# Two score matmul streams of a windowed attention, issued in turn instead of one after the other

## The chip, the core and the metric

One core of one Trainium2 chip runs the whole program in one launch. The metric is the device time of that launch in microseconds; the times below are of three runs. The matrix engine is TensorE (PE in the profile, PEld its weight loads), the others are VectorE (DVE), ScalarE (ACT), GpSimd (POOL) and SyncE (SP, which issues DMAs).

## What is computed

Two transformer layers over x of shape (8, 512, 128). The first two thirds of the work are not touched: layer 0 (differential attention and a quantised linear map) and the attention branch of layer 1. The change lies in the feed-forward branch of layer 1, which is itself a small transformer of depth 6 with 16 heads of 64 and windows of 32 tokens:

```python
for i in range(DEPTH):                       # 6
    x = attn_layer(shift_tokens(x), Wqkv[i], ...) + x
    x = ffn_layer(shift_tokens(x), ...) + x

# local_attention: each window of 32 queries sees its own 32 keys and the 32 before
sim = jnp.einsum('bhwie,bhwje->bhwij', bq, bk2) * QK_SCALE
sim = jnp.where(mask, -jnp.finfo(sim.dtype).max, sim)
attn = jax.nn.softmax(sim, -1)
out = jnp.einsum('bhwij,bhwje->bhwie', attn, bv2)
```

Before the scores, queries and keys are brought to unit length, scaled and rotated.

## The kernel before

The depth loop (`l`) holds an attention part and an FFN part. The attention part goes over 32 tiles (8 sequences of 4 tiles of 128 tokens) with a software pipeline of three stages: `slot(front, mid, back, order)` is written out once for every engine, and in one slot the engines do the *back* half of tile n (scores to output projection), the transposes of queries and keys (*mid*) of tile n+1, and the projections (*front*) of tile n+2. `tiles` runs slots in a loop of 7 iterations of 4 slots, with 4 more written out behind it. So a layer has 32 slots with a back half, 192 in all, and the loop turns 6 times in a layer.

TensorE's order within a slot is fixed by hand: the score block (lines 937 to 950), keys of the front tile (L961), transposes of the exponentials in two halves (L967), values (L975), the weighted sums (L983), queries (L989), transposes of the attention output (L997), the transposes of the next tile's queries and keys (L1004), and the output projection (L1009). In each second slot of four it also transposes the next sequence (L912).

The score block works on two groups of 8 heads. In `qT` and `kT` head 2i lies in partitions 0 to 63 and head 2i+1 in 64 to 127, at the same index i. A half `a` writes PSUM bank 7 (a = 0) or bank 5 (a = 1): one mask matmul of 128 rows and 512 columns in bf16 starts the sums (L942), then 8 heads x 4 windows of fp32 matmuls, each 64 rows x 32 columns of weights over 64 keys, add to them (L948). The four windows write four different groups of 32 partitions. The last of a half raises `s_so`.

What follows on the other engines in the same slot. VectorE: for half 0 and then 1, the row maximum out of PSUM (L1168) and the subtraction (L1170); then the front's key cosines (L1151), sines (L1156), norms (L1161), the reciprocals and products that give Y (L1186 to L1190), and at the slot's end the residual (L1208) and then the query cosines (L1151 again). ScalarE: exp of each half (L1074), squares of the keys (L1079), copies of the transposed exponentials (L1083), values (L1090), squares of the queries (L1094), copies of transposes (L1097, L1100, L1103). GpSimd: the inverse norms (L872 to L877) and the sums and scalings of queries and keys (L881 to L888). Each engine takes its own instructions in order, and semaphores join them; TensorE waits for `s_ex` of half c before it transposes half c (L965).

Of the kernel before, what the change touches and what calls it, by code (L numbers as in the profile page):

```python
# [13 lines left out]
P = 128  # L14
# [6 lines left out]
H = 16  # L21
# [10 lines left out]
DH = 64  # L32
INNER = H * DH
WIN = 32
# [45 lines left out]
def program(nc, x, consts, wqkv0, wproj0, wff0, rows0, wqkv1, wo1, wqkv, wo, qkscale, w1, w2, cols, b2, out):  # L80
    with ExitStack() as outer:
        def sb(name, shape, dt=F32, ctx=outer):
            return ctx.enter_context(nc.sbuf_tensor(name, shape, dt))
# [4 lines left out]
        identb = sb("identb", [P, P], BF16)  # L88
        winb = sb("winb", [P, 2, 2 * WIN], BF16)
# [83 lines left out]
        with ExitStack() as ctx:  # L173
# [44 lines left out]
            with ExitStack() as c2:  # L218
                def sem(name):
                    return scoped(c2, name)  # L220
# [464 lines left out]
        with ExitStack() as ctx:  # L685
# [18 lines left out]
            qT = sb("ls_qT", [P, H // 2, P], F32, ctx)  # L704
            kT = sb("ls_kT", [P, H // 2, WIN + T], F32, ctx)
# [32 lines left out]
            s_so, s_mx, s_sub, s_ex = sem("local_scores"), sem("row_max"), sem("less_max"), sem("local_exp")  # L738
# [40 lines left out]
            def banks(i, n=1):  # L779
                return PS[:, i:i + n, :].rearrange("p b n -> p (b n)")  # L780
# [6 lines left out]
            S_BANK, PT_BANK, O_BANK, W_BANK, X_BANK = (7, 5), (7, 4), 5, 0, 1  # L787
# [113 lines left out]
            def _(pe):  # L901
# [7 lines left out]
                with pe.Fori(0, DEPTH) as l:  # L909
# [15 lines left out]
                    def slot(front, mid, back, order):  # L925
# [7 lines left out]
                        if back:  # L933
                            b, t, n = back
                            n, q = l * TILES + n + 1, t % 2

                        if back:
                            pe.wait_ge(s_qte, n)
                            pe.wait_ge(s_kte, n)
                            for a in range(2):  # L940
                                o = banks(S_BANK[a])
                                pe.matmul(o, identb[:, :], winb[:, 0 if t else 1, :].unsqueeze(1).to_broadcast([P, H // 2, 2 * WIN]),  # L942
                                          start=True, stop=False)
                                r = slice(a * DH, a * DH + DH)
                                for i in range(H // 2):
                                    for w in range(NW):
                                        k0 = t * P + WIN * w
                                        ins = pe.matmul(o[WIN * w:WIN * w + WIN, i * 2 * WIN:(i + 1) * 2 * WIN], qT[r, i, WIN * w:WIN * w + WIN],  # L948
                                                        kT[r, i, k0:k0 + 2 * WIN], start=False, stop=(i == H // 2 - 1))
                                ins.then_inc(s_so, 1)  # L950
                        if front:
                            if ft == 0:
                                pe.wait_ge(s_xe, l * B + fb + 1)
# [6 lines left out]
                            for c in range(2):  # L960
                                ins = pe.matmul(banks(K_BANK + c), rows, WQ[:, INNER + c * 512:INNER + c * 512 + 512], start=True, stop=True)  # L961
                            ins.then_inc(s_k, 1)
                        if back:
                            for c in range(2):
                                pe.wait_ge(s_ex, 2 * n - 1 + c)  # L965
                                for i in range(4):
                                    ins = pe.transpose(banks(PT_BANK[c])[:, i * P:i * P + P], PR[:, (c * 4 + i) * P:(c * 4 + i + 1) * P], ident)  # L967
                                ins.then_inc(s_pt, 1)
                        if front:
# [4 lines left out]
                            for e in range(2):  # L974
                                ins = pe.matmul(banks(V_BANK + e), rows, wv[:, e], start=True, stop=True)  # L975
                            ins.then_inc(s_v, 1)
                        if back:
                            pe.wait_ge(s_pte, 2 * n)
                            pe.wait_ge(s_vb[q], windows(l, b, t))
                            for i in range(H // 2):  # L980
                                for w in range(NW):
                                    at = (i % 3) * 2 * (DH + 1)
                                    ins = pe.matmul(banks(O_BANK + i // 3)[WIN * w:WIN * w + WIN, at:at + 2 * (DH + 1)],  # L983
                                                    PRT[:, i * P + WIN * w:i * P + WIN * w + WIN], VB[q][:, w, :, i, :], start=True, stop=True)
                            ins.then_inc(s_o, 1)
                        if front:
                            pe.wait_ge(s_ve, nf)
                            for c in range(2):
                                ins = pe.matmul(banks(Q_BANK + c), rows, WQ[:, c * 512:c * 512 + 512], start=True, stop=True)  # L989
                            ins.then_inc(s_q, 1)  # L990
                        if back:
# [4 lines left out]
                            for i in range(INNER // P):  # L996
                                ins = pe.transpose(banks(Y_BANK, 2)[:, i * P:i * P + P], Y[:, i * P:i * P + P], ident)  # L997
                            ins.then_inc(s_yt, 1)
                        if mid:
                            for a, at, ready, done in ((0, QT_BANK, s_nq, s_qt), (1, KT_BANK, s_nk, s_kt)):  # L1000
                                pe.wait_ge(ready, nm)
                                for i in range(H // 2):
                                    c = a * INNER + i * P
                                    ins = pe.transpose(banks(at, 2)[:, i * P:i * P + P], A[mq][:, c:c + P], ident)  # L1004
                                ins.then_inc(done, 1)
                        if back:
                            pe.wait_ge(s_yte, n)
                            for i in range(INNER // P):
                                ins = pe.matmul(banks(W_BANK)[:, 0:D], YT[:, i * P:i * P + P], WO[:, i, :], start=(i == 0), stop=(i == INNER // P - 1))  # L1009
                            ins.then_inc(s_w, 1)  # L1010

                    tiles(pe, begin, slot, lambda b: None, prep)

                    def ready(p):
# [312 lines left out]
```

## Time and profile before

| | |
|---|---|
| time, median of 3 runs | 5635.59 us (5633.15 to 5646.27) |
| time of the profiled execution | 5633.29 us |
| its span, first to last instruction | 5631.3 us |
| mean granted TensorE clock | 0.903 of full |
| TensorE matmuls busy | 4707.3 us (84%) |
| VectorE busy | 3589.5 us (64%) |
| ScalarE, GpSimd busy | 2466.6 us (44%), 2512.1 us (45%) |

The page shares the span into 40 slices and gives each engine's busy tenths in each. Groups of instructions are listed with their count, their busy time and the idle time of the engine just before them, with what ended it; "issue" says that the engine waited for nothing that the profile shows. The stage with the score block begins at about 1656 us and ends at about 5525 us, with the FFN parts in it. A fp32 matmul leaves two records of its own, each with a weight load. The end of a matmul is modelled, so the starts are what to go by.

### The profile page before, as it was taken

The numbers are of one execution on the slowest core, as the hardware profiler recorded it, in microseconds if no ns is written. First come the engines' busy times: TensorE is split into PE (matmuls) and PEld (weight loads), VectorE is DVE, ScalarE is ACT, GpSimd is POOL, SyncE is SP. The second block draws the span as 40 slices with busy tenths as digits, with TensorE's granted clock in tenths as the row PEclk, the third lists the DMA queues.
The fourth block names the chain that finished last, engine by engine and source line by source line (L and its number), as shares of the span: only waits on it lengthen the run. The fifth ranks groups of instructions, "written<-read, shape, count | busy, mean of one in ns | idle before, by whom it ended". The sixth has DMA issues, their size and how long they took to land. (4 is left out here: it accounts for less than half of the span.)

```text
span 5631.3 us, 144287 instructions
## 1 busy us (share of the span) xinstructions
PE 4707.3 (84%) x58081; PEld 3028.4 (54%) x58081; DVE 3589.5 (64%) x6107; ACT 2466.6 (44%) x3020; POOL 2512.1 (45%) x3540
## 2 busy tenths in 40 slices
PE   3555567776779998899988999799988999889997
PEld 2333322222236666566655666466665666556664
DVE  6665556655646666566756666566666666656675
ACT  2433433443344444444534444344443444434453
POOL 1000011111146664566626666266654666356671
PEclk9888877887789999999999999999999999989999
DMA  0000000000012221222212222122221222122220
GB/s 27 0 0 0 0 1 0 0 0 0 0 47 71 68 67 47 54 67 67 68 30 71 67 67 65 36 67 67 70 61 38 69 71 67 39 54 70 72 66 22
DMA packets 156765, 246.36 MB, mean 44 GB/s; under 512 B 33488, under 2 KB 50896, under 8 KB 155472
## 3 DMA queue, kind: packets, MB, share of 16 engines
q1 hardware_dynamic: 156240, 238.09, 15.9%
q8 instruction: 485, 7.95, 0.6%
q14 instruction: 40, 0.33, 0.0%
HBM read 20.38 MB, written 2.10 MB: 4 GB/s over the span
## 5 line engine op out<-in xcount | busy, mean ns | idle before, releaser
L1151 DVE TENSOR_TENSOR ls_a<-PS,TC 128x1024 f32<-128x1024 f32 x384 | 467.6, 1219 | 424.4 <-ACT ls_r L1079 424.4
L1074 ACT ACTIVATE ls_q<-ls_q 128x512 f32<-128x512 f32 x384 | 242.0, 630 | 891.1 <-DVE ls_q L1170 891.1
L1161 DVE TENSOR_REDUCE ls_ss<-ls_r 128x16 f32<-128x1024 f32 x384 | 466.2, 1214 | 256.6 <-ACT ls_r L1094 256.6
L1156 DVE TENSOR_TENSOR ls_q<-PS,TS 128x512 f32<-128x512 f32 x768 | 491.1, 680 | 19.5 <-POOL ls_a L881 19.5
L948 PE MATMUL PS<-ls_kT,ls_qT 64*32 64x64 f32 x24576 | 483.0, 233 | 6.8 <-issue 6.7
L948 PEld LDWEIGHTS PS<-ls_kT,ls_qT 64*32 64x32 f32 x24576 | 411.4, 117 | 121.3 <-issue 121.1
L381 POOL TENSOR_TENSOR QT<-MXT,ONE 3x512 bf16<-3x512 bf16 x128 | 146.9, 1148 | 729.6 <-ACT MXT L534 722.4
L961 PE MATMUL PS<-WQ,ls_xsT 128*128 128x512 f32 x768 | 453.1, 720 | 16.6 <-issue 15.3
L872 POOL TENSOR_TENSOR ls_nw<-ls_ss,ls_nw 128x32 f32<-128x32 f32 x192 | 48.3, 252 | 925.0 <-DVE ls_rn L1200 925.0
L881 POOL TENSOR_TENSOR ls_a<-ls_a,ls_q 128x1024 f32<-128x1024 f32 x192 | 451.9, 2354 | 15.0
L884 POOL TENSOR_TENSOR ls_a<-ls_a,ls_q 128x1024 f32<-128x1024 f32 x192 | 453.3, 2361 | 0.0
L983 PEld LDWEIGHTS PS<-ls_vb,ls_q 128*32 128x32 f32 x12288 | 338.0, 110 | 150.4 <-issue 74.6
L1094 ACT ACTIVATE ls_r<-PS 128x1024 f32<-128x1024 f32 x192 | 197.1, 1027 | 498.9 <-PE PS L989 498.9
L653 DVE TENSOR_REDUCE mxs<-PS 128x1 f32<-128x512 f32 x512 | 328.2, 686 | 123.3 <-PE PS L416 116.6
L983 PE MATMUL PS<-ls_vb,ls_q 128*32 128x130 f32 x12288 | 392.7, 280 | 8.7 <-ACT ls_q L1083 8.7
L989 PE MATMUL PS<-WQ,ls_xsT 128*128 128x512 f32 x768 | 384.5, 623 | 14.2 <-ACT ls_vt L1090 14.2
L975 PE MATMUL PS<-WQ,ls_xsT 128*128 128x512 f32 x768 | 372.7, 609 | 20.9 <-DVE ls_a L1151 20.9
L1004 PE MATMUL PS<-CT,ls_a 128*128 128x128 f32 x3072 | 371.8, 274 | 14.2 <-POOL ls_a L886 9.6
L1009 PE MATMUL PS<-WO,ls_r 128*128 128x128 f32 x3072 | 377.8, 276 | 6.7 <-ACT ls_r L1097 6.7
L1168 DVE TENSOR_REDUCE ls_mx<-PS 128x8 f32<-128x512 f32 x384 | 263.1, 685 | 178.0 <-PE PS L948 178.0
L886 POOL TENSOR_TENSOR ls_a<-ls_a,ls_rn 128x1024 f32<-128x1024 f32 x192 | 365.3, 1903 | 15.1
L406 PE MATMUL PS<-identb,PT 128*72 128x128 bf16 x2048 | 159.3, 245 | 247.2 <-DVE PT L613 230.7
(215 smaller groups left out, 9400.6 us busy)
## 6 DMA issues: line engine op xcount, KB each, us to landing
ls_vb<-ls_vt SPq DMA_DIRECT2D x1152, 130.0 KB, 2.4
ls_vb<-ls_vt SPq DMA_DIRECT2D x672, 65.0 KB, 2.0
ls_xs<-XL SPq DMA_DIRECT2D x42, 256.0 KB, 4.0
WQ<-wqkv SPq DMA_DIRECT2D x6, 1536.0 KB, 6.6
ls_vb<-ls_vz SPq DMA_DIRECT2D x96, 65.0 KB
WO<-wo SPq DMA_DIRECT2D x24, 128.0 KB, 6.3
X<-x SPq DMA_DIRECT2D x8, 256.0 KB, 4.5
out<-X SPq DMA_DIRECT2D x8, 256.0 KB, 3.5
```

Source lines behind the costliest of these rows:

```text
L881: pool.tensor_tensor(a4[:, 1], a4[:, 1], b4[:, 1], ALU.add).then_inc(s_ck, 1)
L884: pool.tensor_tensor(a4[:, 0], a4[:, 0], b4[:, 0], ALU.add).then_inc(s_cq, 1)
L948: ins = pe.matmul(o[WIN * w:WIN * w + WIN, i * 2 * WIN:(i + 1) * 2 * WIN], qT[r, i, WIN * w:WIN * w + WIN], kT[r, i, k0:k0 + 2 * WIN], sta ...
L961: ins = pe.matmul(banks(K_BANK + c), rows, WQ[:, INNER + c * 512:INNER + c * 512 + 512], start=True, stop=True)
L975: ins = pe.matmul(banks(V_BANK + e), rows, wv[:, e], start=True, stop=True)
L983: ins = pe.matmul(banks(O_BANK + i // 3)[WIN * w:WIN * w + WIN, at:at + 2 * (DH + 1)], PRT[:, i * P + WIN * w:i * P + WIN * w + WIN], VB[q ...
L989: ins = pe.matmul(banks(Q_BANK + c), rows, WQ[:, c * 512:c * 512 + 512], start=True, stop=True)
L1004: ins = pe.transpose(banks(at, 2)[:, i * P:i * P + P], A[mq][:, c:c + P], ident)
L1009: ins = pe.matmul(banks(W_BANK)[:, 0:D], YT[:, i * P:i * P + P], WO[:, i, :], start=(i == 0), stop=(i == INNER // P - 1))
L1151: nc.vector.tensor_tensor(v4(A[fq])[:, a], src, tab, ALU.mult).then_inc(done, 1)
L1156: ins = nc.vector.tensor_tensor(v4(SW)[:, a, :, lo:lo + h2], src[:, :, hi:hi + h2], TS[:, ft, a, lo:lo + h2].unsqueeze(1).to_broadcast([P, ...
L1161: nc.vector.tensor_reduce(ss[:, fq, a * H:a * H + H], v4(SQ)[:, a], AX.X, ALU.add).then_inc(done, 1)
```

## The change

The mask matmuls of both halves are issued first. Then the loop over heads is outside and the loop over the two halves within it: 4 windows of half 0, 4 of half 1, then the next pair of heads. Each half raises `s_so` after its last matmul, as before.

```diff
                             for a in range(2):
-                                o = banks(S_BANK[a])
-                                pe.matmul(o, identb[:, :], winb[:, 0 if t else 1, :].unsqueeze(1).to_broadcast([P, H // 2, 2 * WIN]),
+                                pe.matmul(banks(S_BANK[a]), identb[:, :], winb[:, 0 if t else 1, :].unsqueeze(1).to_broadcast([P, H // 2, 2 * WIN]),
                                           start=True, stop=False)
-                                r = slice(a * DH, a * DH + DH)
-                                for i in range(H // 2):
+                            for i in range(H // 2):
+                                for a in range(2):
+                                    r = slice(a * DH, a * DH + DH)
                                     for w in range(NW):
                                         k0 = t * P + WIN * w
-                                        ins = pe.matmul(o[WIN * w:WIN * w + WIN, i * 2 * WIN:(i + 1) * 2 * WIN], qT[r, i, WIN * w:WIN * w + WIN],
-                                                        kT[r, i, k0:k0 + 2 * WIN], start=False, stop=(i == H // 2 - 1))
-                                ins.then_inc(s_so, 1)
+                                        ins = pe.matmul(banks(S_BANK[a])[WIN * w:WIN * w + WIN, i * 2 * WIN:(i + 1) * 2 * WIN],
+                                                        qT[r, i, WIN * w:WIN * w + WIN], kT[r, i, k0:k0 + 2 * WIN],
+                                                        start=False, stop=(i == H // 2 - 1))
+                                    if i == H // 2 - 1:
+                                        ins.then_inc(s_so, 1)
```

## Rows read from the trace of the kernel before

**Rows 1.** The page: busy time by engine, and TensorE's tenths of 40 slices.

```profile
PE 4707.3 (84%) x58081; PEld 3028.4 (54%) x58081; DVE 3589.5 (64%) x6107; ACT 2466.6 (44%) x3020; POOL 2512.1 (45%) x3540
...
PE   3555567776779998899988999799988999889997
```

**Rows 2.** Score matmuls: the page's group, then durations ns (min/median/max) of the line.

```profile
L948 PE MATMUL PS<-ls_kT,ls_qT 64*32 64x64 f32 x24576 | 483.0, 233 | 6.8 <-issue 6.7
...
L948 PE MATMUL PS<-ls_kT,ls_qT x24576: 216/216/313, 1656.5 to 5512.1; 64*32 64x64 f32 x200
```

**Rows 3.** Timeline of one tile from 2410.64: start us, us, engine, line [idle before].

```profile
2410.64 0.38 PE L942 MATMUL PS<-winb,identb 128*128 128x512 bf16 x1
2410.95 1.10 PE L948 MATMUL PS<-ls_kT,ls_qT 64*32 64x64 f32 x64
2410.98 0.29 DVE L1208 TENSOR_TENSOR XL<-PS,XL 128x128 f32 x1 [0.66 <-PE PS L1009]
2411.19 1.21 DVE L1151 TENSOR_TENSOR ls_a<-PS,TC 128x1024 f32<-128x1024 f32 x1
...
2412.32 0.68 DVE L1168 TENSOR_REDUCE ls_mx<-PS 128x8 f32<-128x512 f32 x1
...
2413.32 1.98 PE L961 MATMUL PS<-WQ,ls_xsT 128*128 128x512 f32 x4
...
2415.07 0.63 ACT L1074 ACTIVATE ls_q<-ls_q 128x512 f32<-128x512 f32 x1 [0.69 <-DVE ls_q L1170]
2415.14 1.27 PE L967 MATMUL PS<-CT,ls_q 128*128 128x128 f32 x8
...
2421.29 0.41 DVE L1190 TENSOR_TENSOR ls_r<-PS,ls_rc 128x256 f32<-128x256 f32 x1
2421.85 0.41 PE L997 MATMUL PS<-CT,ls_r 128*128 128x128 f32 x2
```

**Rows 4.** Timeline of the next tile: its first matmul, and VectorE's first maximum.

```profile
2426.72 0.38 PE L942 MATMUL PS<-winb,identb 128*128 128x512 bf16 x1
...
2428.20 0.69 DVE L1168 TENSOR_REDUCE ls_mx<-PS 128x8 f32<-128x512 f32 x1 [0.17 <-PE PS L948]
```

**Rows 5.** All waits: engine and line, what for, us in total, times, longest us.

```profile
PE PS L942 <- issue: 83.0, 36, 2.8
```

**Rows 6.** Timelines of two tiles that follow a turn of the loop.

```profile
2391.35 0.38 PE L942 MATMUL PS<-winb,identb 128*128 128x512 bf16 x1 [2.01 <-issue]
...
2392.82 0.69 DVE L1168 TENSOR_REDUCE ls_mx<-PS 128x8 f32<-128x512 f32 x1 [1.91 <-PE PS L948]
...
2393.00 0.68 PE L948 MATMUL PS<-ls_kT,ls_qT 64*32 64x64 f32 x19
...
2394.41 1.50 PE L948 MATMUL PS<-ls_kT,ls_qT 64*32 64x64 f32 x45 [0.74 <-issue]
2395.84 0.50 PEld L961 LDWEIGHTS PS<-WQ,ls_xsT 128*128 128x128 f32 x2 [0.17 <-issue]
...
2529.51 0.38 PE L942 MATMUL PS<-winb,identb 128*128 128x512 bf16 x1 [2.51 <-issue]
2529.81 1.93 PE L948 MATMUL PS<-ls_kT,ls_qT 64*32 64x64 f32 x64
...
2534.08 3.21 PE L961 MATMUL PS<-WQ,ls_xsT 128*128 128x512 f32 x4
2537.12 1.04 PE L967 MATMUL PS<-CT,ls_q 128*128 128x128 f32 x8
```

**Rows 7.** Busy time by stretch, with the granted clock (PEclk).

```profile
2410.60:2458.10 47.50, 47.47 (x768) 33.61 (x767) 35.49 (x57) 25.33 (x32) 35.19 (x52) 1.00 0.30 79
2461.60:2468.20 6.60, 6.50 (x104) 3.94 (x94) 2.76 (x4) 1.26 (x2) 6.52 (x4) 0.50 0.01 2
...
2529.50:2548.00 18.50, 18.49 (x254) 13.14 (x255) 10.57 (x17) 8.09 (x10) 9.58 (x10) 0.82 0.16 42
2598.10:2618.20 20.10, 20.10 (x254) 14.10 (x255) 10.63 (x17) 8.21 (x10) 9.50 (x9) 0.75 0.13 34
```

## What the change does to the time: the prediction

> **What bounds the kernel now.** I read the page first, then the costliest groups, then a timeline of one attention tile in the last stage, and last the tiles after a loop turn. TensorE is busy 84% of the span, and 9 tenths or more in the stage where the change lies [rows 1]; the local score matmuls (L948) are its largest group there, 483 us [rows 2]. That makes the change look promising, and the timeline says otherwise. The reader is to see in [rows 3] that two things are full at once in a tile of about 15.6 to 16.1 us. TensorE issues without a hole: score block (two mask matmuls L942, two halves of L948) from 2410.64 to 2413.32, 2.68 us, then keys L961, and so on. Beside it runs a loop that holds no score matmul: the residual L1208 waits for the output projection L1009 of the tile before; VectorE then does L1151 (query cosines), the first maximum L1168, subtraction L1170, L1168, L1170, back to back; ScalarE's second exponential ends at 2415.70; and only then can TensorE transpose the second half (L967) and go on to L975. L967 lasts 1.27 us there against 1.04 us in [rows 6] where nothing is waited for: 0.23 us of it are the wait for that exponential. On VectorE the same exponential leads through L1079, L1151 and the rest to L1190, which ends at 2421.70, just before L997 starts at 2421.85. So the score block and the loop are level.
>
> **The change, part by part.** Instructions, operands and sums stay the same: 2 L942 and 64 L948 (128 records, as fp32 takes two each) a tile. Only order moves.
>
> (a) Both L942 come first. Before, each costs 0.31 us from its start to that of the first L948 [rows 3]. Full-array bf16 matmuls of 512 columns that follow each other need not let the array run empty between them; 512 columns are four times L948's pair of passes over 64 (55 ns, below), so about 0.22 us. So the first L948 comes at 0.22 + 0.31 = 0.53 us instead of 0.31. The flag for VectorE's first half can't come until that half is done.
>
> (b) The 64-row halves alternate. The trace shows how closely column tiles overlap: 64 records in 1.10 us, of which the last takes 0.22 [rows 2, 3]: 0.88 us, 16 groups of four at 55 ns. At the half clock it is 1.93 - 0.31 = 1.62 us, 101 ns or so a group [rows 2, 6]. It doubles with the clock period, so a group is bound by what streams through the array, not by the issue of instructions. Row halves in turn are nowhere in this trace. Bounds: they overlap fully, all 128 records in 0.88 us; or not at all, 1.76 us. Below nothing is not excluded either, but four column tiles already overlap freely with no cost for changing tile, so I take none. I take the full overlap, since the nearest row (column tiles at one half) shows four of four overlapping. The Trainium skill ("TensorEngine Tiling (Array Packing)", Key Properties) also says that tiles run independently, and that only a change of mode drains the engine; no run here shows it for row tiles.
>
> (c) The first flag moves. Before, the last record of the first half starts at 0.31 + 0.88 = 1.19 us of the tile; with full overlap at 0.53 + 0.88 = 1.41, 0.22 later. In the tile at 2426.72 the maximum waits 0.17 us for the flag and starts at 1.48; in the tile at 2410.64 it starts at 1.68 without waiting, since VectorE comes from L1151 [rows 3, 4]. So it has 0.20 us of slack there, which the 0.22 uses up. The second flag comes 1.1 us sooner but VectorE is still at the first half: worth nothing.
>
> **The sum for full overlap.** TensorE leaves the block 2.68 - 1.56 = 1.1 us sooner (0.53 + 0.88 + 0.15 for the last to drain = 1.56), does the keys, and then waits for the second exponential, whose time the loop pins. In the 150 tiles that don't follow a loop turn the gain is nothing. About 48 of them (those like 2426.72) have the flag 0.22 late; half or more of it is taken by the slack before L975 and L997, I take 0.08: 48 x 0.08 = 4 us lost; 12 tiles at the layers' ends, without new queries and keys, are a plain chain of latencies: 12 x 0.2 = 2 us lost.
>
> The other 42 tiles come after a turn of the loop: 36 where TensorE's first matmul waits for something the profile doesn't show, 83.0 us in all [rows 5], and the 6 first of the layers. Here the clock was granted at half (1.2 GHz) for some 7 us after that wait of 2.0 to 2.5 us [rows 6, 7] (0.50 from 2461.60 to 2468.20), and the block sets the pace: 4.49 us from 2391.35 to 2395.84. But part of that is again a wait for nothing shown: after 64 + 19 records L948 stops and goes on at 2394.41, 3.06 us after the tile's start [rows 6]. I read both waits as instructions being fetched after the jump; the change has as many instructions, so the point stays at about 3.06, the faster order only reaches it sooner, and the remaining 45 records take 45 / 8 x 107 ns = 0.6 us rather than 1.2. The block ends at about 3.06 + 0.6 + 0.15 = 3.8 us instead of 4.49: 0.7 gained. In a turn without a second stop (4.57 us from 2529.51 [rows 6]) the stop would appear, at about 2.9, and the gain is near the same. VectorE's first maximum slips from 1.47 to about 4.0 us of the tile; with 0.69 x 4 + 0.63 the second exponential ends near 7.4, where TensorE has just done the keys (L961, 3.21 us at mostly half clock [rows 6]: 3.8 + 3.3 = 7.1). So I take 0.6 of 0.7: 36 x 0.6 = 22 us; for the 6 first tiles 0.5 each, 3 us. Sum: -22 - 3 + 4 + 2 = -19 us on the profiled 5633.3 us, 5614; that execution lies 2.3 us under the median, so **5616 us**. FFN and the two attentions before are untouched. Between full overlap's own ends, 5590 (the fetched instructions come as soon as they are wanted) and 5640.
>
> **Rivals.** Break-even: 150 tiles x d us of a later flag eat 19 us at d = 0.13, a group of eight at 63 ns rather than 55. So a little missing overlap turns the sign.
>
> *Partial overlap.* Sixteen instructions must pass in 55 ns, where the trace shows eight; if issue or PSUM writes hold the eight tiles to 1.5 times the old pace, the records take 1.17 us, the flag is another 0.29 late, and 150 x 0.29 = 44 us are lost, with turns gaining 0.4 x 36 = 14 and the 6 us above: about 5635.6 + 44 + 6 - 14 = 5672. The skill's measured packing of four row tiles ("TensorE: Matmul & The Clock Gate", Part 3: 3.07 times for four) points this way.
>
> *No overlap: slower.* The halves share the array in turn; the block shrinks by one drain at most, and the first flag comes after 30 of 32 groups: 0.53 + 30 x 0.055 = 2.18 instead of 1.19, 0.99 later, less 0.20 slack where VectorE was late: about 0.8 in 150 tiles, 120 us, less some 5 at the turns: 5750. Each tile's loop runs through L1168, so all of it counts. For it: nothing in the trace has shown two row groups at once; against: the free overlap of column tiles. The same skill page (Part 1) says that matmuls never start closer than about 25 ns; the trace shows 0.88 us / 64 = 14 ns [rows 3], so the trace disagrees, but a floor just under 14 would give this rival's time.
>
> *The clock.* TensorE idles 1.1 us more in every tile, and after a turn it also stops for almost 2 us at the fetch. After the 2.0 to 2.5 us waits the granted clock fell to half; the tile at 2598.10 had it longer (mean 0.75, 20.1 us) than the one at 2529.50 (0.82, 18.5 us) [rows 7]: 1.6 us a time. If all 36 turns went so, 58 us: 5674. Against: the 1.0 of the whole stretch 2410.60 to 2458.10 holds small waits too, none of 1 us though.
>
> **How the numbers follow.** Full overlap 0.40, partial 0.28, none 0.25, clock 0.07. Likeliest: 5616, a hair over 0.3% under the median, and 0.3% (17 us) is about what a measurement of this kernel can tell from no change. Full overlap splits 0.24 faster, 0.14 same, 0.02 slower; the light end of partial overlap gives 0.03 faster and 0.12 same, the rest 0.13 slower; none is slower; the clock case is 0.02 same, 0.05 slower. Faster 0.27, same 0.28, slower 0.45. The likeliest case is a small gain while the cases of a loss hold more chance together, so the range must reach both: 5590 to 5755, leaving out the lower tail of the first case and the upper of the others, under 2 in 10.
>
> **What would show it.** Right: L948 (new line) with 128 records in one row of about 1.1 us at full clock; L1168 starting 1.65 to 1.7 us after the first L942 in every warm tile; the wait of L967 for ScalarE's exponential grown by about 1.1 us; tile lengths still 15.6 to 16.1. Partial or none: that row at 1.4 to 2.0 us, L1168 waiting for TensorE in all tiles, tiles of 16.0 to 16.9. Clock: more stretches granted at half. Wrong altogether: tiles shorter than 15.5 us, which would mean the loop through VectorE isn't what I take it for, or a block after turns that doesn't stop at the 84th record.

## The result and the profile after

Before and after ran in turn, five times each. The median went from 5635.59 us (5625.54 to 5651.88) to 5681.4 us (5674.48 to 5682.55), a ratio of 1.0072 with a 95% interval of 1.0051 to 1.0093: slower by 0.7%, 46 us, where the forecast was 5616. The profiled execution took 5675.67 us, its span is 5673.7 against 5631.3.

The page of the kernel after, to be read beside [rows 1]: busy time of the engines, then two groups of the list (busy us, mean ns | idle before, by releaser). The line numbers have moved by two: L948 is still the scores, L941 the masks, L963 the keys, L969 the transposes of the exponentials, L1170 the maximum, L1076 the exponential.

```profile
PE 4579.6 (81%) x58081; PEld 2885.5 (51%) x58081; DVE 3590.5 (63%) x6107; ACT 2463.7 (43%) x3020; POOL 2511.3 (44%) x3540
...
L1170 DVE TENSOR_REDUCE ls_mx<-PS 128x8 f32<-128x512 f32 x384 | 263.1, 685 | 246.6 <-PE PS L948 246.2
...
L969 PE MATMUL PS<-CT,ls_q 128*128 128x128 f32 x1536 | 257.4, 295 | 156.8 <-ACT ls_q L1076 153.7
```

TensorE did its work in 128 us less and the kernel got longer: it now waits 153.7 us for exponentials, and VectorE waits 246.6 us for scores, where it was 178.0 before. One tile shows how. The timeline of the kernel after, of the tile that answers to [rows 3] (start us, us, engine, line, [idle before]), and the maximum of the next one, that answers to [rows 4]:

```profile
2413.50 0.59 PE L941 MATMUL PS<-winb,identb 128*128 128x512 bf16 x2
...
2414.03 1.79 PE L948 MATMUL PS<-ls_kT,ls_qT 64*32 64x64 f32 x128
...
2415.74 1.98 PE L963 MATMUL PS<-WQ,ls_xsT 128*128 128x512 f32 x4
2415.76 0.69 DVE L1170 TENSOR_REDUCE ls_mx<-PS 128x8 f32<-128x512 f32 x1 [0.50 <-PE PS L948]
...
2417.89 0.66 PE L969 MATMUL PS<-CT,ls_q 128*128 128x128 f32 x4 [0.17 <-ACT ls_q L1076]
...
2419.21 0.65 PE L969 MATMUL PS<-CT,ls_q 128*128 128x128 f32 x4 [0.67 <-ACT ls_q L1076]
...
2430.18 0.59 PE L941 MATMUL PS<-winb,identb 128*128 128x512 bf16 x2
2430.70 1.49 PE L948 MATMUL PS<-ls_kT,ls_qT 64*32 64x64 f32 x128
...
2432.16 0.69 DVE L1170 TENSOR_REDUCE ls_mx<-PS 128x8 f32<-128x512 f32 x1 [0.68 <-PE PS L948]
```

The block, from the first mask to the first key matmul, takes 2.24 us instead of 2.68 in the first of them and 2.05 in the second, so TensorE is earlier at the keys. But VectorE's first maximum comes 2.26 us and 1.98 us after the tile's start, where it was 1.68 and 1.48, and everything behind it follows; TensorE gives its gain back as a wait at L969.

Two more places. The tile after a loop turn that answers to the ones of [rows 6], and what it waits for in total (the view of waits: us, times, longest), both of after:

```profile
2464.76 0.59 PE L941 MATMUL PS<-winb,identb 128*128 128x512 bf16 x2 [2.37 <-issue]
2465.28 1.06 PE L948 MATMUL PS<-ls_kT,ls_qT 64*32 64x64 f32 x83
2467.79 0.94 PE L948 MATMUL PS<-ls_kT,ls_qT 64*32 64x64 f32 x45 [1.46 <-issue]
2468.66 3.05 PE L963 MATMUL PS<-WQ,ls_xsT 128*128 128x512 f32 x4
```

```profile
PE PS L941 <- issue: 78.5, 36, 2.7
...
PE PS L948 <- issue: 41.7, 36, 1.8
```

And the last tile of a layer, which has no keys, values or queries to put into the waits. First the stretches of that tile in the kernel after, then that tile in two layers of the kernel before (stretch, length, busy time (count) of PE, PEld, DVE, ACT, POOL, granted clock, DMA share, GB/s):

```profile
2856.30:2863.40 7.10, 3.65 (x154) 2.58 (x155) 2.96 (x5) 2.34 (x4) 0.00 (x0) 1.00 0.01 2
2863.40:2866.80 3.40, 3.04 (x60) 2.58 (x50) 0.27 (x3) 0.00 (x0) 0.00 (x0) 0.50 0.02 5
...
2870.20:2873.60 3.40, 3.25 (x15) 3.25 (x16) 0.00 (x0) 0.09 (x1) 0.00 (x0) 0.50 0.00 0
```

```profile
2184.30:2199.00 14.70, 9.19 (x228) 7.23 (x225) 4.96 (x12) 3.36 (x5) 0.00 (x0) 1.00 0.01 2
2850.30:2868.60 18.30, 13.20 (x228) 10.44 (x225) 4.96 (x12) 3.36 (x5) 0.00 (x0) 0.72 0.01 2
```

Before, this tile is 14.7 us long in four layers and 18.3 in the two in which the clock was granted at half (1.2 GHz) in it. After, it falls in all six, and the tile takes 18.2 to 19.8 us.

Where the 42.4 us of span come from, tile by tile. A tile is measured from its first mask matmul to the next one's, and grouped by its place in the loop of four:

| tiles | number | mean before, us | mean after, us | total, us |
|---|---|---|---|---|
| after a loop turn, or first of a layer | 42 | 19.03 | 17.92 | -46.7 |
| second of four | 42 | 16.09 | 16.56 | +20.0 |
| third of four | 42 | 15.61 | 16.12 | +21.3 |
| fourth, with the wait of the turn | 36 | 18.10 | 18.31 | +7.6 |
| fourth, no turn behind it | 6 | 15.63 | 15.96 | +2.0 |
| next to last three of a layer | 18 | 15.78 | 16.44 | +11.8 |
| last of a layer | 6 | 15.9 | 19.0 | +18.6 |
| FFN parts, and where the stage starts | | | | +8 |

The first row holds two kinds. The 36 tiles after a turn went from 19.06 to 18.16 us, 32 us in all; the six first of a layer from 18.87 to 16.46, 14.5 us in all. Of these six, four ran their whole score block at the half clock in the profile of before and three in that of after, so a part of the 14.5 us is the clock.

### The profile page after: what moved, and what is told of

Read it like the earlier page. It is cut to its first block and busy times, and to the rows that moved or that the text cites. A ratio compares the mean times of both kernels' runs of the same rounds, so it can differ in the third digit from the quotient of the medians.

```text
span 5673.7 us, 144287 instructions
## 1 busy us (share of the span) xinstructions
PE 4579.6 (81%) x58081; PEld 2885.5 (51%) x58081; DVE 3590.5 (63%) x6107; ACT 2463.7 (43%) x3020; POOL 2511.3 (44%) x3540
## 3 DMA queue, kind: packets, MB, share of 16 engines
q1 hardware_dynamic: 156240, 238.09, 15.9%
## 5 line engine op out<-in xcount | busy, mean ns | idle before, releaser
L1076 ACT ACTIVATE ls_q<-ls_q 128x512 f32<-128x512 f32 x384 | 241.8, 630 | 965.1 <-DVE ls_q L1172 965.1
L963 PE MATMUL PS<-WQ,ls_xsT 128*128 128x512 f32 x768 | 431.2, 689 | 20.0 <-issue 14.0
L1170 DVE TENSOR_REDUCE ls_mx<-PS 128x8 f32<-128x512 f32 x384 | 263.1, 685 | 246.6 <-PE PS L948 246.2
L991 PE MATMUL PS<-WQ,ls_xsT 128*128 128x512 f32 x768 | 386.1, 626 | 14.1 <-ACT ls_vt L1092 14.1
L977 PE MATMUL PS<-WQ,ls_xsT 128*128 128x512 f32 x768 | 372.5, 608 | 20.9 <-DVE ls_a L1153 20.9
L969 PE MATMUL PS<-CT,ls_q 128*128 128x128 f32 x1536 | 257.4, 295 | 156.8 <-ACT ls_q L1076 153.7
L1011 PEld LDWEIGHTS PS<-WO,ls_r 128*128 128x128 f32 x3072 | 368.1, 196 | 8.3 <-ACT ls_r L1099 8.3
L886 POOL TENSOR_TENSOR ls_a<-ls_a,ls_rn 128x1024 f32<-128x1024 f32 x192 | 365.4, 1903 | 15.0
L888 POOL TENSOR_TENSOR ls_a<-ls_a,ls_rn 128x1024 f32<-128x1024 f32 x192 | 365.1, 1902 | 0.0
```

The costliest lines, as they stand in the source:

```text
L886: pool.tensor_tensor(a4[:, 0], a4[:, 0], scale(0), ALU.mult).then_inc(s_nq, 1)
```

## The experiments

Unless it says otherwise a ratio is against the kernel before, with its 95% interval. "First maximum" is VectorE's first row maximum of a tile, counted from that tile's first mask matmul; warm tiles are the second, third and fourth of each four, which run at the full clock; the three numbers are means over the second, third and fourth tiles of four (before: 1.68, 1.47, 1.66 us; after: 2.14, 2.01, 1.98).

**1. The late flag alone.** The kernel before, with its order of matmuls, but half 0 raises its flag only from the first head of half 1:

```diff
-                                ins.then_inc(s_so, 1)
+                                    if a and i in (0, H // 2 - 1):
+                                        ins.then_inc(s_so, 1)
```

> The order of before; only the flag for half 0 is raised later, by the first head of half 1, about 0.58 us after its own last matmul (the changed kernel's first maximum starts 0.33 to 0.54 us later than before's). TensorE's work is untouched. Theory (the first flag's lateness goes straight into a loop through VectorE, tile after tile): first maximum at about 2.05 us of every tile instead of 1.47 to 1.68, tiles 0.4 to 0.45 us longer, 150 tiles: 60 us, so 5690 to 5700. Rival (the loss comes from how TensorE takes its instructions, the clock or the fetch after a turn, and VectorE has room): within 15 us of before.

5735.46 us, ratio 1.0182 (1.0160 to 1.0205). TensorE's stream is that of [rows 3], and only VectorE moves (timeline of this kernel; L1169 is its maximum):

```profile
2577.86 0.38 PE L942 MATMUL PS<-winb,identb 128*128 128x512 bf16 x1
2578.17 1.10 PE L948 MATMUL PS<-ls_kT,ls_qT 64*32 64x64 f32 x64
...
2579.90 0.69 DVE L1169 TENSOR_REDUCE ls_mx<-PS 128x8 f32<-128x512 f32 x1 [0.28 <-PE PS L948]
```

The first maximum is at 2.04 us in all three classes, that is 0.36, 0.57 and 0.39 later, and the tiles are 0.38, 0.55 and 0.40 us longer (16.46, 16.16, 16.03). So a later first flag alone makes the loss, one to one, with no cushion. It costs more than the whole change because after turns it loses 13 us (19.33 us a tile) where the change gains 47; the last tile fell to the half clock in all six layers in both. The loss was larger than the 55 to 65 us that I expected: of the 112 us between the profiled executions 74 lie in the 186 tiles ahead of the layers' last, 19 in the last tiles, 12 in the FFN parts, and 7 are a stage that began later.

**2. The masks first, the halves still one after the other.**

```diff
                                           start=True, stop=False)
+                            for a in range(2):
+                                o = banks(S_BANK[a])
                                 r = slice(a * DH, a * DH + DH)
```

> Part one of the change alone: both mask matmuls first, then the halves one after the other. Theory: the first flag comes 0.22 us later, which is the 0.20 us of slack; TensorE leaves the block 0.2 us sooner: within 15 us of before, tiles of 15.6 to 15.7 us. Rival (two masks in front already cost the 45 us): 5670 or more.

5650.06 us, ratio 1.0028 (1.0014 to 1.0043). The first maximum is at 1.69 us everywhere: unchanged where VectorE was late anyway, 0.21 later in the third tile of four, which got 0.19 longer (15.80). The turn tiles (with the first of each layer) got 0.63 shorter (18.40) with no row half beside another: more than half of the gain of the change there (1.11) comes from the masks alone. The time is at the edge of the 15 us that I expected, and what holds it up lies elsewhere: the last tile of a layer fell to the half clock in all six layers here too, and the last four tiles of the layers cost 24 us more than before.

**3. Two heads of half 0 for one of half 1**, so that the first flag comes earlier than in the change, with some overlap kept:

```diff
+                            at = [0, 0]
+                            for a in (0, 0, 1, 0, 0, 1, 0, 0, 1, 0, 0, 1, 1, 1, 1, 1):
+                                i = at[a]
+                                at[a] += 1
```

> Both masks first, then two heads of half 0 for one of half 1 until half 0 is done, then the rest of half 1. Same instructions. Theory (after TensorE's queue of ready instructions is used up, matmuls come about 8 ns apart, which is enough for half 0 at full pace and a part of half 1): half 0 is done at 1.4 to 1.5 us of the tile, first maximum at 1.7 to 1.75, block end as with the change (keys at 1.95 to 2.05 us); the gain after loop turns stays; 5610 to 5640. Rival (alternating row halves slows half 0 whatever the ratio): first maximum at 1.9 or later, 5660 or more.

5644.16 us, ratio 1.0022 (1.0008 to 1.0037). First maxima 1.83, 1.77, 1.76; tiles 16.25, 15.89, 15.74; turn tiles 18.12. All of it lies between experiment 2 and the change, as it must if only the place of the first flag and the length of the block count. The 186 tiles ahead of the layers' last add up to 9 us less than before; the last tiles took it back, with 17.9 to 18.9 us in five layers and 16.2 in one. The first maximum was to come at 1.7 to 1.75 us and the time to be 5640 at most, so this is a near miss.

**4. VectorE's query cosines ahead of the residual**, in the kernel before, so that VectorE is free sooner:

```diff
+                        if front:
+                            cosines(0, Q_BANK, s_aq)
                         if back:
                             dve.wait_ge(s_w, n)
...
-                        if front:
-                            cosines(0, Q_BANK, s_aq)
```

> The order of before on TensorE; on VectorE the query cosines of the front tile go ahead of the residual, in whose wait for TensorE (0.63 to 0.66 us) they fit. Theory (loop through VectorE): the first maximum no longer comes behind the cosines and starts at about 1.47 us in every tile instead of 1.68 in two of three; L967 no longer waits; TensorE's own work is then the bound at about 15.4 to 15.5 us a tile: 10 to 25 us faster than before. Rival (TensorE alone bounds): within 5 us.

5629.33 us, ratio 0.9996 (0.9981 to 1.0012): no change in time, where I expected 10 to 25 us. The first maximum is at 1.47 us in all tiles, the second tile of four is 0.16 shorter, the fourth 0.14, the third the same: where the maximum comes sooner the tile is shorter, which is the converse of experiment 1. The 186 tiles together are 28 us shorter in the profiled execution, but its stage began 22 us later than in that of before and the last tile fell to half clock in three layers instead of two. Where the stage begins differs by up to 44 us between profiled executions of kernels whose work up to there is the same, so only the tiles carry this reading, not the total.

**5. The key matmuls between pieces of the score block.** Does the array or the supply of instructions limit the block? The change, with one key matmul after the first two pairs of heads and one after the next two; all the work is the same:

```diff
+                                if front and i in (2, 4):
+                                    c = i // 2 - 1
...
+                                    ins = pe.matmul(banks(K_BANK + c), rows, WQ[:, INNER + c * 512:INNER + c * 512 + 512], start=True, stop=True)
```

> The changed kernel with the two key matmuls of the front tile put into the block: one after the heads i = 0 and 1 of both halves (32 score matmul records), one after i = 2 and 3 (32 more), the rest behind. It tells two causes of the slow second part of the block apart. Theory (instructions come about 8 to 9 ns apart once the ready ones are used up; while a key matmul of 0.86 us runs, ready ones pile up again): each of the first two parts and the first 32 records of the third start within 0.24 us, as the first 32 do in the changed kernel. Rival (row halves hinder each other after the start, in PSUM or in reading): the second and third parts show 0.28 us or more for 32. The time of the whole is of no interest, since the flags come later: 5700 or more.

It is far slower (6251 us in its one execution); VectorE waits 605.2 us for scores there. What it is for is the pace (timeline of this kernel: L962 scores, L955 keys):

```profile
2506.91 0.45 PE L962 MATMUL PS<-ls_kT,ls_qT 64*32 64x64 f32 x32
2507.29 1.13 PE L955 MATMUL PS<-WQ,ls_xsT 128*128 128x512 f32 x2
2508.35 0.45 PE L962 MATMUL PS<-ls_kT,ls_qT 64*32 64x64 f32 x32
2508.73 1.13 PE L955 MATMUL PS<-WQ,ls_xsT 128*128 128x512 f32 x2
2509.79 0.86 PE L962 MATMUL PS<-ls_kT,ls_qT 64*32 64x64 f32 x64
```

By the starts of the records, the first 32 after a long matmul begin within 0.238 us, in all three places and in all 126 warm tiles: mostly 6 to 7 ns apart, 8 records per 55 ns, full overlap of the row halves. The last 32 of the third piece take 0.40 us. In the change the same: the first 32 records begin within 0.238 us, and the next three lots of 32 take 0.37, 0.31 and 0.35 (medians), so that 128 begin within 1.27 us instead of 0.88 (in the second tiles of four, as the one at 2413.50 above, within 1.39). As the same heads go fast when a long matmul stands before them and slow when other score records do, neither the array nor the writes to PSUM limit them. What is used up is a stock of 32 records with their 32 weight loads; I read it as TensorE running ahead of its instructions. The Trainium skill ("TensorE: Matmul & The Clock Gate", Architectural detail: the array is 16× 32×32, not 1× 128×128) gives TensorE's queue as 64 instructions; the 32 + 32 in the fast stretch agree. How it is filled up again stays open: a stock that is filled at the later pace (about 11 ns a record) while it is used at 6.9 ns should last for more records than it holds, and no run shows why the pace falls right behind the 32nd.

**6. The last two tiles of a layer filled.** The change, with mask matmuls into a bank that nobody reads, 25 in the last tile and 21 in the one before, in the places where TensorE waits:

```diff
+                                for _ in range(k):
+                                    pe.matmul(banks(V_BANK), identb[:, :], winb[:, 0, :].unsqueeze(1).to_broadcast([P, H // 2, 2 * WIN]),
+                                              start=True, stop=True)
...
+                                fill((8, 3)[c])
```

> The changed kernel; in the last two tiles of each layer, which have no new keys, values and queries, TensorE runs mask matmuls into a PSUM bank that nobody reads while it would wait (8, 3, 3, 7 and in the last tile 4). The output is the same. Theory (about 30 of the 42 us lost lie at the layers' ends, because TensorE's idle pieces there grew from 0.9 to 2.1 us and the clock was granted at half in all six layers instead of two): no half clock from tile 30 to the end of tile 31, last tile to FFN 14.8 to 15.5 us instead of 18.2 to 19.8: 5650 to 5660. Rival (the half clock there comes whatever TensorE does): 5675 to 5690.

5652.3 us, ratio 1.0039 (1.0024 to 1.0053): 29 us under the change by the two medians, about 19 by the two ratios, each against the kernel before at its own time. More work for TensorE, and the last tile went to 15.2 us in all six layers, at 2.4 GHz throughout (stretch of this kernel that answers to 2856.30 to 2873.60 above):

```profile
2855.40:2870.60 15.20, 14.07 (x253) 8.88 (x251) 4.94 (x12) 3.36 (x5) 0.00 (x0) 1.00 0.01 2
```

The warm tiles are as in the change (16.59, 16.13, 15.97). The last four tiles of the layers are 37 us shorter than in the change; experiment 9 tells how much of that is the change's own. So most of the layer ends' loss is the clock, and TensorE's idle time there is what brings it.

**7. Small masks.** To take the masks' cost off the path: experiment 3's order and 4's cosines, and the masks as eight matmuls of 64 rows and 32 columns behind one short full one, so that they overlap as the scores do:

```diff
+                            pe.matmul(banks(S_BANK[0])[:, 0:2 * WIN], identb[:, :], winb[:, 0, :], start=True, stop=True)
...
+                                for w in range(NW):
+                                    r = slice(a * DH, a * DH + DH)
+                                    pe.matmul(banks(S_BANK[a])[WIN * w:WIN * w + WIN], identb[r, a * DH:a * DH + WIN],
```

> Built from the two-to-one order: the two mask matmuls of 128 rows become eight of 64 rows x 32 columns on the same eight tiles as the scores (behind one short full-array matmul that takes the wait), so nothing drains between masks and scores and both masks stream at once; and VectorE's query cosines go ahead of the residual. Theory: the first flag comes at about 1.25 us, first maximum at about 1.5 us in every tile (before: 1.47 to 1.68), keys at 1.8 to 1.9 us; warm tiles of 15.4 to 15.6 us, the gain after turns stays (about 1 us in 42 tiles): 5580 to 5610. Rival (mask matmuls on small tiles bring back a mode change or use up the ready instructions): first maximum at 1.8 or later and 5640 or more.

5624.14 us, ratio 0.9978 (0.9965 to 0.9990). The first score record starts at 0.35 us instead of 0.53, the last at 1.82 instead of 2.02; first maxima 1.60, 1.56, 1.56; tiles 16.03, 15.67, 15.54. I expected 5580 to 5610. Two things are missing: the last tile fell to the half clock in five layers of six, and the turn tiles gained 0.68 us (18.35), not 1.

**8. Small masks and filled ends** (7 and 6 together).

> The small-mask kernel (two heads of half 0 for one of half 1, small masks, cosines ahead of the residual) with the last two tiles of each layer filled as in the run before. Theory: its own last tile cost 18.4 us in five layers of six, as the changed kernel's; filling takes it to 15.2 us and tile 30 from 16.2 to 15.0: 20 to 28 us less than 5624, so 5596 to 5605. Rival (filling helps only where the masks of 512 columns stand together): 5615 or more.

5598.99 us, ratio 0.9942 (0.9925 to 0.9959). Halves in turn are part of a faster kernel once the flag is held early and the layer ends are kept from the half clock. Whether the mixed order adds anything to it isn't shown: no run has the small masks and the early cosines with the halves one after the other, and experiment 2, where the halves follow each other, already took the turn tiles to 18.40.

**9. The kernel before with filled ends.**

> The kernel before with the same filling. It tells how much of the 29 us that filling gave the changed kernel is the change's own loss. Theory (before had the half clock in the last tile in two layers of six in its profile, and a short stretch in tile 30 in all): 6 x 0.9 us in tile 30 and about 2 x 3.6 less: 5620 to 5628. Rival (filling is worth the same everywhere, so the layers' ends are no part of the change's loss): 5600 to 5610.

5623.1 us, ratio 0.9980 (0.9969 to 0.9990). The filling alone is worth 0.2% where two of six ends had fallen: 11 us in the last four tiles of the layers. With the ends filled in both, the change (experiment 6) is only 5 us longer there than the kernel before, against 30 without. The other 0.4% of experiment 8 belong to the block and the cosines together.

**10. The loop of seven turns written out**, in the kernel before, on all engines:

```diff
-                with eng.Fori(0, B - 1) as g:
+                for g in range(B - 1):
```

> The kernel before with the loop over 7 x 4 tiles written out, so that no engine jumps within a layer; instructions and waits are otherwise the same. It tests what the waits with no releaser after a turn are. Theory (instructions are being fetched after the jump): neither the 2.0 to 2.5 us before the first mask nor the stop after 83 score records come any more, the clock stays full through a layer: 36 x (2.5 + 3.4) = 210 us less: 5410 to 5440. Rival (the waits belong to a sequence's first tile, not to the jump): within 1% of before.

5426.68 us, ratio 0.9623 (0.9605 to 0.9642). No wait of L942 for issue is left of the 83.0 us of [rows 5], turn tiles and fourth tiles take 15.98 and 15.51 us instead of 19.03 and 18.10, and TensorE is busy without a hole in the middle of a layer (stretch of four tiles that begins where a turn was; the last column but two is the clock):

```profile
2455.50:2518.00 62.50, 62.48 (x1022) 44.58 (x1021) 47.28 (x76) 33.29 (x42) 46.63 (x69) 1.00 0.28 74
```

So the stops after a turn were the jump's. That they are instructions which weren't there yet is a reading; for it speaks that the second stop comes behind the 83rd record in either order of the block. The Trainium skill ("Runtime: NRT & Kernel Launch", Instruction fetch mechanics) says that a taken branch breaks the sequential prefetch, and that the engine stalls when the target isn't in the stretch of instructions already fetched; the trace agrees, with 36 waits of up to 2.8 us, the second stop, and the half clock they bring.

**11. Everything together**: 8 with the loop written out.

> All of it together: small masks in the two-to-one order, cosines ahead, last tiles filled, loop written out. With no turns left the change's gain there (about 1 us in 42 tiles) is gone too, and what stays is the warm tile of 15.5 to 15.6 us: about 25 to 35 us under the written-out kernel (192 x 0.08 and the layers' ends): 5385 to 5410.

5429.14 us, ratio 0.9627 (0.9608 to 0.9646). I expected 25 to 35 us under experiment 10; it is the same. The view of waits of this kernel names a new one, where experiment 10 has none on its score line, and the timeline shows it (L964 scores, L954 small masks, L979 keys):

```profile
PE PS L964 <- issue: 24.8, 20, 1.7
```

```profile
2457.54 0.41 PE L954 MATMUL PS<-winb,identb 64*32 64x512 bf16 x8
2457.76 1.66 PE L964 MATMUL PS<-ls_kT,ls_qT 64*32 64x64 f32 x120
2461.00 0.32 PE L964 MATMUL PS<-ls_kT,ls_qT 64*32 64x64 f32 x8 [1.58 <-issue]
```

The block stops after 108 to 122 records for 1.1 to 1.9 us, in the tiles 9, 10, 22 and 23 (counted from 0) of nearly every layer, the same places in the code each time, and the keys stop once more for 1.1 to 1.4 us in tile 8 of all six. There is no jump there. By the same reading the faster block runs out of instructions in a straight line too. The second, third and fourth tiles of four get longer than those of experiment 10 (the second 16.32 against 15.95), which eats what the layer ends gain (last tile 14.8 us in all six against 18.2 in three of six).

## Why the prediction was wrong

The step that failed is (b), the full overlap of the two row halves: 128 records in 0.88 us were forecast, and 1.27 us were measured. It makes the first flag late, and the step behind it, (c), priced a late flag too low. Together the warm tiles cost 51 us instead of 4; with the flag where full overlap would have put it (experiment 2) they cost 10. A second term failed beside them: the layers' last tiles, put at 2 us, cost 30.

**The bound: right.** TensorE and a loop through VectorE are level, and the block's length isn't what a warm tile hangs on. Experiments 1 and 4 moved the first maximum alone, later and sooner, and the tiles followed; in the change the block got 0.6 to 0.75 us shorter in the median of each class (0.44 in the tile shown) and the tiles longer. TensorE's wait at L969 is where the gain went, as said: 0.84 us in the tile shown against 0.23 before, so grown by 0.6 and not by 1.1.

**(a) The masks first: right.** The first score record starts at 0.525 us in the warm tiles of after, 0.53 was said.

**(b) The overlap: the failed step.** I took all 128 records in 0.88 us because a group "is bound by what streams through the array, not by the issue of instructions". That holds at half clock, where 128 records of the first tiles begin within 1.75 us, 8 per 107 ns; and for the first 32 records at full clock. From there something else binds, by experiment 5 neither the array nor PSUM, and the 128 records take 1.27 us. The row used for the inference, column tiles at the old pace, was bound by what streams while it asks for half as many instructions in a nanosecond; it said nothing on the double. The rival of partial overlap named the issue of instructions as a cause (with PSUM writes, which it isn't), took 1.5 times the old pace (1.17 us) and gave 5672. Measured are 1.39 times the old pace and 5681; that the two times lie so near is partly luck, since this rival had neither the layer ends nor the larger gain at the turns in its sum.

**(c) The flag: sized far too small.** It was to come 0.22 later, of which VectorE's lateness would take 0.20, and only 48 tiles would lose 0.08. It came so that the first maximum is 0.46, 0.54 and 0.33 later in the three classes, and the tiles are 0.48, 0.51 and 0.34 longer. Two things are in it: (b)'s 0.39 us, and the missing cushion. Experiment 2, whose flag is the one that I forecast, cost the third tile of four 0.19 for 0.21, not 0.08. The "slack before L975 and L997" that I had read out of [rows 3] doesn't exist. In the warm tiles the sum said +4 and it was +51 (20.0, 21.3, 7.6 and 2.0). About 10 of them are the price of the flag at full overlap (experiment 2); the other 41 come with the missing overlap.

**The turns: right in kind, too small in size.** The block after a turn stops after 83 records; in the tile shown it goes on 3.03 us after the tile's start (forecast 83, about 3.06) and is over at 3.90 (3.8), in others between 3.4 and 4.2. As forecast the second stop appeared where there was none: 14 of the 36 turns had it before, all 36 have it after. And the order buys only what lies between the stops. But each of the 36 tiles gained 0.90 us, not 0.6, and the six first of a layer 2.4, not 0.5: their half clock also got shorter, 4.2 us a tile over the 42 instead of 7.4. Of the 36, 5 had none at all, 13 had 3.4 us and 18 had 6.8, where before 30 had 6.8 and six 10.2. Why the clock was granted sooner isn't shown. The stretch of half clock that answers to the second row of [rows 7] is 3.4 us long here and begins 2.7 us after the tile's start instead of ahead of most of its block (stretches of after):

```profile
2464.70:2467.40 2.70, 1.58 (x85) 1.02 (x85) 0.00 (x0) 0.00 (x0) 2.60 (x3) 1.00 0.03 8
2467.40:2470.80 3.40, 3.01 (x48) 1.80 (x49) 2.03 (x4) 0.63 (x1) 3.32 (x3) 0.51 0.03 5
```

So -46.7 against the forecast's -25. The rival on the clock had this place the wrong way round. That the waits are the jump's, which I had only read, experiment 10 shows; that they are its fetch stays a reading.

**The layer ends: next to nothing in the sum.** I gave the last two tiles of each layer 0.2 us each, as a plain chain. The last four cost 30 us (11.8 and 18.6 in the table), and most of it is the clock: filled in both kernels (experiments 6 and 9), they differ by 5 us. The clock rival looked at the turns only; the mechanism it names, that a TensorE idle for longer is granted less, is right at the layer ends. In the last tile it waits 2.1 us at L969 where it waited 0.85 before; with the masks first alone (experiment 2) it waits 1.4 us, and there all six layers fell too. The order of before is itself at the edge: with that wait of 0.85 us it fell in two layers of six, in the profiles of experiments 4 and 10 in three. Timelines of before, then after:

```profile
2853.92 1.06 PE L967 MATMUL PS<-CT,ls_q 128*128 128x128 f32 x4 [0.85 <-ACT ls_q L1074]
```

```profile
2860.37 0.66 PE L969 MATMUL PS<-CT,ls_q 128*128 128x128 f32 x4 [2.10 <-ACT ls_q L1076]
```

The sum with what was measured: -47 at the turns, +51 in the other warm tiles, +30 at the layer ends, +8 elsewhere, 42 us in all. Had the overlap been full, the flag would have come as in experiment 2, whose second, third and fourth tiles together lost 10 us rather than the 4 of the sum, and whose layer ends lost 24. An estimate from these, with the turns and the rest as in the change, is -47 + 10 + 24 + 8, about -5 us: the overlap alone would not have brought the 19 us. No run has it.

## What to carry to other kernels

Before work on one engine is made faster, look for who waits for its first result, and price the delay of that result at one to one in every iteration unless a row shows who absorbs it. A pace that was measured in a stream bound by the array says nothing of the pace at twice the instructions per nanosecond. And a shorter block ahead of an unchanged wait makes the engine idle for longer: look at the granted clock in the sparsest stretches first, at a section's last iterations, and not only where it is low already.

## What the runs showed of the hardware

- Matmuls of 64 rows and 32 columns on all eight tiles of the array start 8 per 55 ns, 6.9 ns each on the mean, for 32 records (0.238 us), the two row halves fully beside each other, at 2.4 GHz. The 96 behind them come about 11 ns apart; all 128 begin within 1.27 us. Behind a long matmul the first 32 are fast again (experiment 5). The Trainium skill ("TensorE: Matmul & The Clock Gate", Part 1, Wait — 56ns, not 53.3ns?) has 25 ns as the least distance between starts; this case's traces are at 6.9 and 14 ns.
- Two full-array bf16 matmuls of 512 columns in a row cost 0.525 us up to the next record, against 0.31 for one. One short full one and eight of 64 rows and 32 columns cost 0.35 us.
- The turn of the loop costs TensorE 2.3 us at once (83.0 us over 36), often a second stop after 83 records of the score matmuls, and then several us of half clock: 211 us over 36 turns by the medians of experiment 10 and of the runs of before beside it. Without jumps dense small matmuls also stop at fixed places in the code, for 1.1 to 1.9 us (experiment 11).
- In the changed kernel, filling TensorE's waits with matmuls whose results nobody reads made the last tile of a layer 3.8 us shorter on the mean, with the clock at 2.4 GHz throughout (experiment 6).
